# GNN layer pair with segment maximum on one core: the one-hot rows of the second merge made by a GpSimd comparison in place of stored bytes

## The reference

```python
msg = x[src] @ W_msg + edge_attr @ W_edge
agg = jax.ops.segment_max(msg, dst, num_segments=N)   # 0 where a node has no edge
h   = leaky_relu(agg + x @ W_root + b)
...
out = layernorm(x + h2)       # h2: the second layer's h, over the 96 features
```

## Time and profile before

| | us |
|---|---|
| median of three runs | 1866.52 |
| the three runs | 1862.57, 1866.52, 1878.78 |
| the profiled execution | 1874.13 |
| its span in the trace | 1872.3 |

### The profile page before, as it was taken

One profiled execution on the slowest core, in us unless ns is written; L12 is line 12 of the kernel. 1 busy time (PEld: TensorE's weight loads), 2 busy tenths in 40 slices (PEclk: granted clock), 3 DMA queues, 4 the chain that ended last, 5 costly groups with the idle time before them and its releaser, 6 DMA issues.

```text
span 1872.3 us, 37110 instructions
## 1 busy us (share of the span) xinstructions
PE 1525.2 (81%) x11422; PEld 1355.2 (72%) x11422; DVE 1315.3 (70%) x2385; ACT 1080.9 (58%) x2450; POOL 1089.0 (58%) x1454
## 2 busy tenths in 40 slices
PE   3998888888889999896889899988987767676663
PEld 2677777777779888885777777777777666576653
DVE  2677677667766655554667777767636789999998
ACT  2354544444543555563555555555527788888887
POOL 6777777767710000004777777777657788675653
PEclk9999999999999999998999999999989899988887
DMA  7778998889875788895878888888767899999996
GB/s 137 212 206 259 285 268 263 263 254 261 261 248 163 239 264 275 284 290 170 223 224 228 238 223 235 233 226 241 205 222 214 248 288 305 296 297 295 294 300 174
DMA packets 505022, 459.13 MB, mean 245 GB/s; under 512 B 348553, under 2 KB 412340, under 8 KB 504836
## 3 DMA queue, kind: packets, MB, share of 16 engines
q1 hardware_dynamic: 444118, 321.15, 60.0%
q0 software_dynamic: 30976, 57.72, 12.3%
q10 hardware_dynamic: 29742, 77.88, 10.6%
HBM read 283.25 MB, written 173.37 MB: 244 GB/s over the span
## 4 chain that ended last, share of the span: by engine, by line
PE 30%; DVE 24%; DMA 20%; POOL 15%; issue 9%; ACT 1%; SPq 1%; DVEq 0%; POOLq 0%; ACTq 0%
PE ps L584 19%; DMA onehot_bytes<-arena_hold 14%; POOL arena_hold L410 12%; DVE stats L953 5%; DMA arena_hold<-nodes,src_perm 4%; DVE arena_hold L896 4%; DVE arena_hold L951 4%; PE ps L495 4%; DVE arena_hold L948 4%; POOL onehot L443 3%; PE ps L463 2%; PE ps L486 2%; DVE arena_hold L882 2%; PE ps L456 2%; DVE arena_hold L971 1%
## 5 line engine op out<-in xcount | busy, mean ns | idle before, releaser
L584 PE MATMUL ps<-arena_hold,onehot 128*128 x4688 | 614.4, 293 | 174.7 <-POOL onehot L443 142.7
L584 PEld LDWEIGHTS ps<-arena_hold,onehot 128*128 128x128 f32 x4688 | 584.1, 206 | 205.3 <-issue 204.2
L410 POOL DMA_INDIRECT arena_hold<-nodes,src_perm x392 | 370.0, 944 | 459.9 <-SPq L377 340.7
L495 PEld LDWEIGHTS ps<-w_root,onehot 97*128 97x128 f32 x3136 | 402.4, 194 | 100.9 <-issue 99.0
L410 POOL DMA_INDIRECT arena_hold<-in_x_dram,src_all x392 | 375.1, 957 | 143.7 <-issue 115.2
L495 PE MATMUL ps<-w_root,onehot 97*128 97x128 f32 x3136 | 418.9, 277 | 0.0
L443 POOL CAST onehot<-keep 128x256 f32<-128x256 uint8 x588 | 302.3, 562 | 117.4 <-PE ps L584 71.6
L648 ACT COPY arena_hold<-ps 128x384 f32<-128x384 f32 x392 | 187.9, 479 | 277.3 <-PE ps L495 275.0
L698 ACT COPY arena_hold<-ps 128x384 f32<-128x384 f32 x392 | 166.7, 477 | 200.3 <-PE ps L584 200.2
L882 DVE TENSOR_TENSOR_SCAN arena_hold<-keep,arena_hold,ps 96x512 f32<-96x512 bf16 x196 | 247.6, 1263 | 42.1 <-PE ps L463 41.8
L896 DVE TENSOR_TENSOR onehot<-count,rel 128x1024 f32<-128x1024 bf16 x147 | 179.5, 1222 | 126.9 <-PE ps L584 126.0
(11 more groups left out here) (99 smaller groups left out, 1160.9 us busy)
## 6 DMA issues: line engine op xcount, KB each, us to landing
root<-arena_hold ACTq DMA_DIRECT2D x196, 384.0 KB
arena_hold<-root SPq DMA_DIRECT2D x196, 384.0 KB, 4.6
nodes<-arena_hold SPq DMA_DIRECT2D x98, 384.0 KB, 3.0
arena_hold<-nodes SPq DMA_DIRECT2D x98, 384.0 KB
arena_hold<-in_x_dram SPq DMA_DIRECT2D x97, 384.0 KB
arena_hold<-in_x_dram SPq DMA_DIRECT2D x48, 768.0 KB, 8.1
out_dram<-arena_hold SPq DMA_DIRECT2D x48, 768.0 KB, 4.7
onehot_bytes<-arena_hold SPq DMA_DIRECT2D x147, 128.0 KB
```

Source lines behind the costliest of these rows:

```text
L410: nc.gpsimd.indirect_dma_start(out=gathered[t.ring][0:t.p, i, 0:D], out_offset=None, in_=table_in, in_offset=bass.IndirectOffsetOnAxis(ap= ...
L495: last = nc.tensor.matmul(no_ps[m % 2][:, i * P:(i + 1) * P], nodes_t[m % NODE_RING][0:D + 1, i * P:(i + 1) * P], w_root[0:D + 1, layer * ...
L584: nc.tensor.matmul(ps_bytes[:, bass.ds(place_at, SLOT)].bitcast(F32), onehot[:, k % NS, i, :], rows_from(t)[:, bass.ds(word, SLOT)].bitcas ...
```

## The change

The bytes go: no comparison into bytes in the first edge phase, no stores, no loads, no casts, no buffers for them, and no wait of TensorE for `bytes_made`. In the second merge GpSimd makes each one-hot matrix by one instruction on 128x128 elements, with a column of `rel` as its per-partition scalar. Of the waits around it the one for the seeded groups and the one for `stepped` stay.

```diff
-            def load_bytes(q):
...
-            pool.wait_ge(scanned, 2 * NE - 2)
-            load_bytes(0)
-            pool.wait_ge(scanned, 2 * NE)
-            load_bytes(1)
             pool.wait_ge(no_full, 2 * NG)
             for k in range(NBATCH):
                 if k % 2 == 0:
                     pool.wait_ge(seeded[1], ...)
                     pool.sem_inc(opened, 1)
-                pool.wait_ge(bytes_in[k // 2 % 2], DMA * (k // 4 + 1))
                 if k >= NS:
                     pool.wait_ge(stepped[1], BATCH * (k - NS + 1))
-                for i in range(0, BATCH, PIECE):
-                    last = nc.gpsimd.tensor_copy(onehot[:, k % NS, i:i + PIECE, :]..., bytes_back(k, 1)[...])
+                for i in range(min(BATCH, T - k * BATCH)):
+                    at = k * BATCH + i
+                    last = nc.gpsimd.tensor_scalar(onehot[:, k % NS, i, :], count[:], rel[:, at:at + 1], None, ALU.is_equal)
                 last.then_inc(grown, 1)
-                if k % 2 and k + 3 < NBATCH:
-                    load_bytes((k + 3) // 2)
...
-                if t.layer == 0 and t.g >= BYTES_AT:
-                    pe.wait_ge(bytes_made, byte_batches(t.g).stop)
...
-            def make_bytes(k):
-                if k >= 2:
-                    dve.wait_ge(bytes_stored[k % 2], DMA * (k // 2))
-                compare(bytes_out[:, k % 2, :]..., k, count_ps).then_inc(bytes_made, 1)
...
-                        if g == BYTES_AT:
-                            then(nc.vector.tensor_copy(count_ps, count[:]))
-                        for k in byte_batches(g):
-                            make_bytes(k)
...
-            def store_bytes(k):
-                sp.wait_ge(bytes_made, k + 1)
-                sp.dma_start(onehot_dram[k // 2][...], bytes_out[:, k % 2, :]).then_inc(bytes_stored[k % 2], DMA)
```

More of the change, by code:

```diff
@@ L25 @@
 BATCH = 8
-PIECE = 2
 RING = 8
@@ L36 @@
 ROWS_ON = 64
-BYTES_AT = 15
 TABLES_TAKE = 3
@@ L82, in gnn @@
         keep_dram = nc.dram_tensor("keep_row", (E,), BF16, kind="Internal").ap()
-        onehot_dram = nc.dram_tensor("onehot_bytes", (-(-NBATCH // 2), P, 2 * BATCH * P), U8, kind="Internal").ap()
         def table(a, s):
@@ L91, in unit_of @@
             return table(a, s)[:, h * UB * D:(h + 1) * UB * D]
-        ARENA = max(2 * UNIT_RING * UB * D + (EDGE_RING + 4) * GE + 2 * BATCH * P // 4, UNIT_RING * UB * D + 5 * RI * D)
+        ARENA = max(2 * UNIT_RING * UB * D + (EDGE_RING + 4) * GE, UNIT_RING * UB * D + 5 * RI * D)
         arena_hold = sb("arena_hold", [P, ARENA + CH * D + P - D], F32)
@@ L128, in gnn @@
         assert HG == UG and BATCH == 2 * C and NODE_RING == 2 * NS and EDGE_RING == 4
[L129 to L134, removed]
         flat = arena_hold[:, ARENA:]
@@ L169, in gnn @@
         et_ps, nt_ps, no_ps, em_ps, eb_ps = bank[0], bank[2:4], bank[4:6], (bank[1], bank[6]), bank[7]
-        count_ps = eb_ps[:, C * D:C * D + P]
         slot = ps[:].rearrange("p (b j k) -> p b j k", b=8, j=C)
@@ L198, in gnn @@
         no_full, root_read, root_stored = sem("no_full"), sem("root_read"), sems("root_stored", UNIT_RING)
-        primed, made, bytes_made, grown, opened = (sem(n) for n in ("primed", "made", "bytes_made", "grown", "opened"))
-        bytes_stored, bytes_in = sems("bytes_stored"), sems("bytes_in")
+        primed, made, grown, opened = (sem(n) for n in ("primed", "made", "grown", "opened"))
         stepped, seeded, evacuated = sems("stepped"), sems("seeded"), sems("evacuated")
@@ L221, in node_groups @@
             return range(at * NG // span, after * NG // span)
-        def byte_batches(g):
-            span = NE - BYTES_AT
-            return range((g - BYTES_AT) * NBATCH // span, (g + 1 - BYTES_AT) * NBATCH // span) if g >= BYTES_AT else range(0)
         unit_loads = {}
@@ L288, in load_nodes @@
                     sp.dma_start(to[0:(rows - full * GE) // C, full, :, :], at).then_inc(block_in[u % UNIT_RING], DMA)
-            def store_bytes(k):
-                sp.wait_ge(bytes_made, k + 1)
-                sp.dma_start(onehot_dram[k // 2][:, k % 2 * BW:(k % 2 + 1) * BW], bytes_out[:, k % 2, :]).then_inc(bytes_stored[k % 2], DMA)
             def edge_phase(layer):
@@ L309, in edge_phase @@
                         load_nodes(layer, u)
-                    if layer == 0:
-                        for k in byte_batches(g - EDGE_RING):
-                            store_bytes(k)
                 for u in unit_loads.get((layer, NE), ()):
                     load_nodes(layer, u)
-                if layer == 0:
-                    for g in range(NE - EDGE_RING, NE):
-                        for k in byte_batches(g):
-                            store_bytes(k)
             def load_root(layer, u):
@@ L374, in _ @@
                 sp.wait_ge(nodes_stored[k], 2 * DMA * ((NSB + 2 - k) // 3))
-            for i in range(2):
-                sp.wait_ge(bytes_stored[i], DMA * ((NBATCH + 1 - i) // 2))
             sp.sem_inc(ready, 1)
@@ L438, in _ @@
                     pool.sem_inc(opened, 1)
-                pool.wait_ge(bytes_in[k // 2 % 2], DMA * (k // 4 + 1))
                 if k >= NS:
                     pool.wait_ge(stepped[1], BATCH * (k - NS + 1))
-                for i in range(0, BATCH, PIECE):
-                    last = nc.gpsimd.tensor_copy(onehot[:, k % NS, i:i + PIECE, :].rearrange("p t n -> p (t n)"), bytes_back(k, 1)[:, 0, i * P:(i + PIECE) * P])
+                for i in range(min(BATCH, T - k * BATCH)):
+                    at = k * BATCH + i
+                    last = nc.gpsimd.tensor_scalar(onehot[:, k % NS, i, :], count[:], rel[:, at:at + 1], None, ALU.is_equal)
                 last.then_inc(grown, 1)
-                if k % 2 and k + 3 < NBATCH:
-                    load_bytes((k + 3) // 2)
         @block.tensor
@@ L898, in compare @@
                     rel[:, k * BATCH:k * BATCH + n].rearrange("p (t a) -> p t a", a=1).broadcast_to([P, n, P]), ALU.is_equal)
-            def make_bytes(k):
-                if k >= 2:
-                    dve.wait_ge(bytes_stored[k % 2], DMA * (k // 2))
-                compare(bytes_out[:, k % 2, :].rearrange("p (t n) -> p t n", n=P), k, count_ps).then_inc(bytes_made, 1)
             def edge_phase(layer):
```

## The result

| | before | after |
|---|---|---|
| median, us | 1868.9 (4 runs) | 2174.94 (4 runs) |
| lowest and highest, us | 1862.57 to 1878.78 | 2169.27 to 2175.44 |
| span of the profiled execution, us | 1872.3 | 2173.6 |

The ratio is 1.162, with a 95% interval of 1.158 to 1.166. The change makes the kernel slower, as forecast, but by 306 us and not by 58, and the time lies above the stated range of 1825 to 2050.

A forecast was written before the change was run, and what follows sets the result against it. Bounds differ by stage: byte stores and comparison in the first edge phase; merge matmuls and casts, then VectorE's finish, in the second merge. Edge phase 32 us shorter, merge 90 longer: 1866.5 + 58 gives 1924 us, range 1825 to 2050.

The forecast's parts named there:

- rival 1: Second merge: comparison as cheap as the affine select, p 0.22 to 0.25, VectorE bounds it, about 1817 us; chance 0.22.
- rival 3: Whole kernel: the longer merge and shorter edge phase cancel, p from 0.26 to 0.28; chance 0.08.
- rival 4: First edge phase keeps its length because transfers, not bytes, slow it; with p = 0.32 gives 1956 us; chance 0.06.
- Rival 2: Second merge: scalar as dear as an operand, p = 0.50, 2135 us; chance 0.14 including what lies between 0.38 and it.
- the price p: Second merge: time of one 128x128 GpSimd comparison, taken as 0.32 us, 1172 times, 375 us.
- the upper bound of 0.50: Second merge: highest comparison price, twice the affine select's 282 ns for a second operand, less some overlap, 0.50 us.
- Holding: Second merge: VectorE's two long finish instructions (L948, L951) hold up GpSimd for their whole time, 179 us.
- The wait and the register read between batches: Second merge: GpSimd's cost before a batch, 0.2 us at 74 of the batches, 15 us.
- the tail: End of the second merge: from the last comparison to the end of the span, 24 us.
- The edge phase: First edge phase: without bytes the gathers set the pace, 21.3 us of ring stall and 10.3 of lag go, 32 us.
- The lag behind it: End of first edge phase: last gather to first priming matmul falls from 26.5 to the second layer's 16.1 us.
- The break-even: Whole kernel: the comparison price at which the change alters nothing, 1172 p = 503 + 32 - 218, p = 0.27 us.

The follow-up runs named there:

- the run without them: The changed kernel with the finish's leaky ReLU and residual (VectorE's two long instructions) each replaced by a one-element copy: 2039.17 us.
- the run of that part alone: The kernel before with bytes neither made nor stored, the second merge still loading and casting as many bytes of a node table: 1845.45 us, ratio 0.986.
- The copies: The changed kernel with a plain copy of `count` in place of each GpSimd comparison, so all one-hots are wrong: 1883.2 us.
- the run with eight forms: The changed kernel with the eight matrices of a batch made by eight different instructions (comparison, immediate, addition, copy, other types, 64 elements): 2137.98 us.

## Why the prediction was wrong

**The direction and the mechanism were right.** GpSimd paces the second merge, is busy for over 90% of it, all others wait for it, and the first edge phase becomes shorter. Rivals 1 and 3, cheap or cancelling, are out, and so is rival 4. Rival 2 came nearest with 2135 us, in part by luck: its p of 0.50 is still too low, and its holding and waits are too high.

**The step that failed is the price p.** "I take 0.32 us" had to be 0.577. That is 1172 x 0.257 = 301 us, while the whole error is 243 (301 us more span against 58). It lies above the upper bound of 0.50 too. Both bounds came from instructions of another kind, a cast and an affine select. A cast takes 0.8 ns an element, the operation with a scalar 2.5. The affine select ran in one size only, so its rate is not known; at 128 columns it is half as long. The upper bound doubled it for a second operand, but the column is only 0.07 us. The slow part was one that no row of before showed: even with an immediate the operation takes 0.53 us. A bound for an operation that a trace doesn't contain has to allow for another rate per element, not only for other fixed parts.

**Holding: 179 forecast, 132 measured.** That it is those two instructions was right, as the run without them shows. But a comparison that has run for 0.2 us or more when VectorE starts is not held. The one that is held starts on average 0.26 us into VectorE's instruction of 1.78 us and ends 0.47 us after it, and it would have taken 0.61 anyway: 1.4 us for each of the 96 holds. The wait and the register read between batches cost 0.3 us and not 15, with 4.5 us elsewhere, and the tail was 17.5 and not 24. These together gave back 63 us of the 301, and the smaller saving of the edge phase and the stages between took 5: 243.

**The edge phase: 32 forecast, 27.6 measured,** 26.7 in the run of that part alone. The last gather starts 17.6 us earlier and not 21.3: 6.4 us of waits for the ring stay from 105 to 500 us. The lag behind it shrinks from 26.5 to 16.5 us, as forecast. One reading of this part does not hold, though nothing in the sum rests on it: the prediction has TensorE busier in the first edge phase than in the second, and by the earlier trace rows its share is 87% in the first and 88% in the second. VectorE's is larger in the first, 71% after 69.

**The break-even was wrong too, though it decided nothing.** The prediction put it at p = 0.27. The copies, at 0.24, take 1883 us in a single run: no faster than before (a median of 1871 beside it), with the edge phase's gain inside. So at that price rival 1's 1817 would not have come. With a GpSimd that is nearly fast enough there are waits for TensorE (101 us here) beside the holding, and a sum of totals does not see them.

## What to carry to other kernels

When a change puts an operation on an engine where the trace has never shown it, bound its price by elements as well as by instructions, and let the range follow that bound: with 1172 of them every 0.01 us was 12 us. A sum of an engine's work, holds and tail served once that engine never paused: with the measured price the prediction's own sum is 63 us above the measured stretch of 831, 3% of the whole time. Near the break-even it was too low. Before work that is waiting for a transfer is moved elsewhere, try whether more buffers take the wait away: here they gave the edge phase's whole gain and none of the merge's cost.

## What the runs showed of the hardware

- On GpSimd, `tensor_scalar` over 128x128 takes 0.53 us with an immediate and 0.60 with a column, an addition as much as a comparison, bfloat16 as much as float32; over 64 columns it takes 0.44, and a copy of 128 columns 0.29 (all in the run with eight forms). A cast takes 0.41 over 256 columns and 0.62 over 512.
- Of two comparisons of one form in a row the next starts after 0.577 us; between two different forms in the run with eight, 0.67 us (L401 to L402) was seen.
- While one of VectorE's two long instructions (128x1536, two SBUF inputs, 1.8 us) ran, the comparison that GpSimd started did not end; it ended some 0.47 us after it, 96 times. One that had run for 0.2 us or more before ended as usual, in 0.7 us at most. VectorE's normalisations with scalars (128x96) held comparisons by 0.02 us on average and 0.12 at most.
- TensorE, fed a batch every 3.4 us, with a pause in nearly every one, was granted 0.98 from 1500 us on. Fed a batch every 4.5 or 4.6 us it was granted 0.77, with holds in the feed and without.
